# Graph layers over a 4096 by 4096 matrix: spills moved from SyncE's queue to GpSimd's, late loads placed between them, quadrants loaded in the order 0, 2, 1, 3

## The reference, cut to what matters

```python
def reference(x, adj, L0_gnn_W, L0_gnn_B, L1_gnn_W):      # x 4096x128, adj 4096x4096, W 128x128, float32
    h = max(layernorm(x), 0)
    msg = h @ L0_gnn_W + L0_gnn_B
    sens = exp(-(1/adj - 1)**2 / 0.5)                     # mu = 1, sigma = 0.5
    x = x + where(adj < 1, sens, 0) @ msg                 # first layer: every block of adj, weighted
    h = max(layernorm(x), 0)
    A = adj + I
    d = sum(A, axis=1) ** -0.5                            # row sums of adj
    x = x + relu((d[:, None] * A * d[None, :]) @ (h @ L1_gnn_W.T))   # second layer: every block again
    return x
```

## Time and profile before

| | us |
|---|---|
| median of 3 runs | 627.53 (626.89 to 627.85) |
| the profiled execution's own time | 632.89 |
| its span in the trace | 631.1 |

### The profile page before, as it was taken

One profiled execution on the slowest core, in us unless ns is written; L12 is line 12 of the kernel. 1 busy time (PEld: TensorE's weight loads), 2 busy tenths in 40 slices (PEclk: granted clock), 3 DMA queues, 4 the chain that ended last, 5 costly groups with the idle time before them and its releaser, 6 DMA issues.

```text
span 631.1 us, 4420 instructions
## 1 busy us (share of the span) xinstructions
PE 537.5 (85%) x1509; PEld 243.6 (39%) x1509; DVE 485.1 (77%) x555; ACT 466.0 (74%) x306; POOL 39.6 (6%) x68
## 2 busy tenths in 40 slices
PE   2446896969877998779769999979999999999995
PEld 2133432323322443334324444434444444444442
DVE  2799977789759899989989979986799849202056
ACT  2286878789967969999999969992999777920010
POOL 0241500000000000000000000000000000101100
PEclk9997998879888999989979999979999999999998
DMA  7999999999999959999999999999699951295623
GB/s 151 197 277 272 277 335 278 277 265 245 313 300 265 202 102 303 307 233 188 306 304 201 203 212 282 270 266 197 236 224 219 233 126 67 93 376 226 236 60 75
DMA packets 87193, 145.14 MB, mean 230 GB/s; under 512 B 4225, under 2 KB 78210, under 8 KB 78210
## 3 DMA queue, kind: packets, MB, share of 16 engines
q1 hardware_dynamic: 82130, 108.15, 75.2%
q0 software_dynamic: 5040, 36.70, 16.2%
HBM read 106.04 MB, written 38.80 MB: 230 GB/s over the span
## 4 chain that ended last, share of the span: by engine, by line
PE 42%; DVE 21%; ACT 14%; DMA 12%; issue 7%; SPq 4%; DVEq 0%
PE acc L377 13%; DMA raw<-in_adj_dram 12%; PE mix L399 11%; PE mix L390 11%; DVE kept L648 9%; DVE wt L663 4%; ACT wt L528 3%; ACT wt L533 3%; ACT wt L538 3%; SPq L281 3%; ACT wt L547 3%; DVE wt L669 2%; DVE rowpart L656 2%; PE acc L399 2%; PE side L399 1%
## 5 line engine op out<-in xcount | busy, mean ns | idle before, releaser
L377 PE MATMUL acc<-wt,msg 128*128 128x512 f32 x512 | 242.0, 617 | 4.7 <-ACT wt L547 4.7
L648 DVE STREAM_TRANSPOSE kept<-raw 128x2048 f32<-128x2048 f32 x64 | 147.6, 2306 | 42.9 <-DMA raw<-in_adj_dram 31.4
L377 PEld LDWEIGHTS acc<-wt,msg 128*128 128x128 f32 x512 | 98.6, 199 | 134.1 <-issue 124.3
L528 ACT ACTIVATE wt<-wt 128x2048 f32<-128x2048 f32 x64 | 121.9, 1905 | 38.1 <-DVE wt L663 38.1
L663 DVE SCALAR_TENSOR_TENSOR wt<-kept 128x2048 f32<-128x2048 f32 x64 | 146.5, 2288 | 1.5
L533 ACT ACTIVATE wt<-wt 128x2048 f32<-128x2048 f32 x64 | 121.6, 1900 | 0.4
L390 PE MATMUL mix<-kept,support 128*128 128x512 f32 x224 | 106.2, 620 | 13.0 <-DVE kept L648 6.5
L547 ACT ACTIVATE wt<-wt 128x2048 f32<-128x2048 f32 x52 | 98.8, 1899 | 0.0
L538 ACT ACTIVATE wt<-wt 128x2048 f32<-128x2048 f32 x52 | 98.7, 1898 | 0.0
L399 PE MATMUL mix<-late,support 128*128 128x512 f32 x200 | 89.7, 592 | 0.0
L656 DVE TENSOR_REDUCE rowpart<-raw 128x16 f32<-128x4096 f32 x20 | 87.6, 4379 | 0.0
(11 more groups left out here) (87 smaller groups left out, 260.8 us busy)
## 6 DMA issues: line engine op xcount, KB each, us to landing
raw<-in_adj_dram SPq DMA_DIRECT2D x128, 512.0 KB, 12.5
adj_t_spill<-kept SPq DMA_DIRECT2D x35, 1024.0 KB, 13.4
late<-adj_t_spill POOLq DMA_DIRECT2D x27, 1024.0 KB, 10.9
raw<-adj_t_spill POOLq DMA_DIRECT2D x8, 1024.0 KB, 6.2
x<-in_x_dram SPq DMA_DIRECT2D x32, 64.0 KB, 7.5
out_dram<-kept SPq DMA_DIRECT2D x32, 64.0 KB, 1.8
w_sb<-in_L_gnn_W_dram SPq DMA_DIRECT2D x1, 64.0 KB
late<-in_L_gnn_W_dram SPq DMA_DIRECT2D x1, 64.0 KB
```

The source lines that it names most:

```text
L377: mm = nc.tensor.matmul(acc0[:], msg[:, col(u) * T + k, :], wt[:, u % WTS, k, :], start=(first and k == 0), stop=(last and k == T - 1))
L528: nc.scalar.activation(v, v, ACT.Ln, bias=LN_GUARD).then_inc(ln_done, 1)
L648: nc.vector.transpose(dst, src).then_inc(turned, 1)
```

## The change

Three things. The spills leave SyncE's queue: GpSimd issues them, in the order of the units. SyncE's program keeps the loads of x, the adj loads and the stores of the result, and the loop over units becomes a plain loop over pairs; what an adj load waits for stays the same. GpSimd's program becomes a loop over the units: the spill of unit u, then (at units 0, 2 and 4) a portion of `support`, then those late loads whose `load_unit` is u. `load_unit(j)` is two units behind the unit at which PE takes the job that had the buffer before, and 16, 17 and 18 for the first three late loads, which have no job before them. The four quadrants of a pair are issued in the order 0, 2, 1, 3 in place of 0, 1, 2, 3. No arithmetic changes and no bytes are added.

```diff
@@ new helpers
+def load_unit(j):
+    before = slot_before(j)
+    if before is None:
+        return 2 * G + j
+    return first_unit(before) + 2
+
+def first_unit(j):
+    return [u for u in sorted(JOBS) for _ in JOBS[u]][j]
@@ SyncE
-                for q in range(Q):
+                for q in (0, 2, 1, 3):
                     sp.dma_start(raw[q * B:(q + 1) * B, n % RAW], ...
-            for u in range(UNITS):
-                if spills(u):
-                    sp.wait_ge(turned, u + 1)
-                    store(u)
-                if u % 2 == 1 and u // 2 + RAW < PAIRS:
-                    load(u // 2 + RAW)
+            for n in range(RAW, PAIRS):
+                load(n)
@@ GpSimd
+            def store(u):
+                pool.wait_ge(turned, u + 1)
+                pool.dma_start(spill[u // G, col(u)], ...).then_inc(spilled[u % KEPT], 16)
-            for j, (r, c) in enumerate(LOADED):
+            for u in range(UNITS):
+                if spills(u):
+                    store(u)
+                if u in (0, 2, 4):
+                    make_h0(u // 2 + 1)
+                for j in range(len(IN_TURN)):
+                    if load_unit(j) == u:
+                        load_late(j)
+            for j in range(len(LOADED)):
+                if j >= len(IN_TURN) or load_unit(j) >= UNITS:
+                    load_late(j)
```

## The result

| | us |
|---|---|
| before, median of 4 runs | 627.61 (626.89 to 627.85) |
| after, median of 4 runs | 639.88 (636.11 to 641.68) |
| ratio, 95% interval | 1.0179 (1.0136 to 1.0222) |
| profiled execution, before and after | 632.89 and 641.68 |

What follows compares the result with a forecast made beforehand. DMA was taken to bound the kernel up to unit 38, then PE and ACT. Terms -4.7 and +1.6 gave -3.1 us, so the median 627.53 becomes 624.4; forecast's range 620.5 to 626.2, 8 in 10 612 to 637.

Steps and rivals of the forecast that it cites:

- What bounds the kernel: Whole kernel: DMA sets the pace through transposes and adj loads up to unit 38 (323 us), then PE and ACT.
- a us is a us: Up to unit 38: a us saved or lost at a transpose moves the end by a us.
- Part 1: First two late loads, moved behind units 16 and 17: load for unit 8 freed of 4.9 us, returning about 70 us later.
- Part 2: Quadrant order of adj loads: four rate rises per pair in place of two, 0.6 us less, 9.9 in place of 10.5.
- Part 3: Spills on their own queue: one more spill in front of each load, +2.5 us once; mixing price taken as 0.
- the term for groups 3 and 4: Loads for units 28, 32 and 38, where spills stop and begin again: +1.6 us, bounds 0 and +5.
- -4.7 was forecast for unit 24: Up to unit 22, kept by unit 24: 12 pairs at -0.6 us make -7.2, plus 2.5 for the extra spill.
- Crowding wins: Rival at adj loads beside spills up to unit 38: slower, 641 or 635 us; chance of slower in all 0.29.
- Of its two ways the second: The rival's case where the new order saves nothing and groups 3 and 4 cost 5 us: +7.5, so 635.

Runs made afterwards that it cites:

- experiment 1: The kernel before with only the quadrants in the order 0, 2, 1, 3, spills still on SyncE's queue: 622.57 us, ratio 0.9898.
- experiment 4: The kernel before with only the late loads' times changed to those of the changed kernel, spills still on SyncE's queue: 628.73 us, ratio 1.0003.
- experiment 6: The changed kernel with the 14 spills of groups 3 to 7 back on SyncE's queue in their old places: 627.87 us, ratio 0.9982.
- experiment 9: The kernel before with quadrant order 0, 2, 1, 3 and the 14 spills of groups 3 to 7 on GpSimd's queue: 632.86 us, ratio 1.0063.
- experiment 10: The changed kernel with spills issued by ScalarE on its own queue, late loads staying with GpSimd: 636.5 us, ratio 1.0123.
- experiment 11: The kernel before with quadrant order 0, 2, 1, 3 and the first four late loads held until units 12, 22, 23, 24 are transposed: 619.24 us, ratio 0.9822.
- experiment 7: The changed kernel with the spill area laid out so that spills and late loads move in pieces of 2 KB, not 8: 639.76 us, ratio 1.0166.

## Why the prediction was wrong, step by step

**What bounds the kernel: right up to unit 38.** Between before and after a us lost at a transpose up to there is one at the end: unit 40 is 8.8 us late and so is the last one, and the spans differ by 8.8. The exchange is not always one for one, though. The order alone gained 8.0 us at unit 38 and 10.3 at the end. PE at unit 38, before and then in experiment 1:

```profile
325.62 6.15 PE L390 MATMUL mix<-kept,support 128*128 128x512 f32 x8 [6.06 <-DVE kept L648]
317.63 3.70 PE L390 MATMUL mix<-kept,support 128*128 128x512 f32 x8 [1.46 <-DVE kept L648]
```

Before, PE had stood 6.06 us, its granted clock from 324 to 328 us was 0.50 (1.2 GHz), and eight matmuls took 6.15 us. In experiment 1 it had stood 1.46 us, the clock was 1.00 (2.4 GHz), and the same eight took 3.70. So some 2.4 us more hang on the wait before unit 38 than the wait itself, and "a us is a us" left this out. After pays it too (5.93 us), so it drops out of the 8.8. Experiment 4, whose profiled execution is near its median, doesn't pay it (3.70 us): its unit 38 is 0.7 us earlier than before and its end 4.0. The profiled execution of before, 5.4 us above its median, is thus partly slow for this, which is one reason why the profiled executions differ by 8.8 us and the medians by 12.3. Whether the other executions of before pay it is not known.

**Part 1: its own sum right, its setting wrong.** The wait of unit 8 went (-4.4 us in place of 4.9), and placing alone moves the time by nothing (experiment 4). But "over the whole DMA-bound stretch" assumed that the stretch stays bound by DMA. It did not: with the lead won, DVE set the pace and DMA time at 124 to 130 us went unused. And "come back about 70 us later" named the four late loads and not what they would meet: four spills in the same 20 us on the same queue, with the load for unit 20 in flight beside it. That was the wait of 16.25 us.

**Part 2: right in mechanism, too large per pair.** Predicted -7.2 us by unit 22; alone it measured -5.2 there, -6.1 at unit 24 and -8.0 at unit 38, and 6.3 us on the median (experiment 1: ratio 0.9898). The rise at every boundary is there; the mean rate alone is 206 GB/s, where 9.9 us a pair needs 212.

**Part 3: the step that failed.** "One more spill in front of each load than before: +2.5 us, once, not per pair, since every earlier load is moved by the same." The exchange rate behind it was right: packets go one for one (729 to 709 from 160 to 175 us), which leaves a load 49 GB/s, a quarter of its 200 where a fifth was said; turns of several pieces at a time, which would have halved the price, are not seen. The price of mixing was near the zero that was taken (29.0 us of work in 28). The count was wrong. "Once" holds where each load is issued early and only queues. It fails where a load is issued late, because it waits for its buffer or for row sums, and has a fixed hour to land. Before unit 30 the single queue let two spills run first in the gap (418 GB/s) and kept the next two behind the load; the second queue let those two cross it, 5.1 us by the rate and 5.5 by the trace. Unit 38 repeats it. The prediction priced the loads for units 28, 32 and 38 and never asked about that for unit 30; for unit 38 it counted one spill fewer in front, where two now cross. So the term for groups 3 and 4, +1.6 in the sum with bounds 0 and +5, measured +9; and it wasn't before unit 28, as said, but before units 30 and 38. The rest of the miss lies earlier: -4.7 was forecast for unit 24 and -0.2 came, which is the first loss and the smaller gain per pair. With both, -4.7 + 1.6 = -3.1 became -0.2 + 9.0 = +8.8.

**The sum by measured terms**, by ratios times 628: the order -6.4 (experiment 1); spills of groups 0 to 2 on a second queue with the late loads among them +5.3 (experiment 6 less experiment 1); spills of groups 3 to 7 on it +10.4 (experiment 9 less experiment 1). In all +9.3, where the ratio 1.0179 makes +11.2. With the other half of groups 3 to 7, after less experiment 6 (+12.4), the sum closes by itself and proves nothing, so the 2 us between are the error of adding parts, and lie within the intervals. The rival "Crowding wins" gave the right side and nearly the time (635 and 641), by luck, with a mechanism that is hardly there: at 150 to 178 us the mixing had no price, and from 160 to 175 rather a gain (5.17 / 0.414 + 0.73 / 0.200 = 16.1 us of work in 15). Only from 248 to 256 us, where the load for unit 30 begins, do the rows leave room for one (0.76 / 0.414 + 1.10 / 0.200 = 7.3 us of work in 8). Of its two ways the second, the upper bound in groups 3 and 4, was the nearer. What the rows of before could have told: SyncE's order shows spills behind every load in flight, so the question at each late-issued load was "which transfers that stood behind it will now cross it?", and not how many spills there are in front on average.

**Open.** Why the order gives 3.3 us in the changed kernel and 6.3 in the old (the two runs of the changed kernel can't tell 3.3 from a gain near 6 or near none; the clock at unit 38 may be a part, since experiment 1 escapes its price and after doesn't); and how the 3.4 us between experiment 10 and after divide.

## What to carry to other kernels

The order of transfers in one first-in-first-out queue is a priority: a transfer behind a load can use the gap after it but doesn't slow it down (before, with two spills queued behind it, the load for unit 30 moved some 1.55 MB in 8 us; beside them, 1.10). Before moving transfers to a second queue, list for each load with a deadline which of them stood behind it and will now cross it, and charge their whole time to it. Deferred transfers go where the trace shows the DMA engines at rest or the next deadline far off, and not in a row with others (experiment 11). And read shares of two queues only in a window in which both have work: over a longer one the mean mixes sharing with running alone.

## What the runs showed of the hardware

Alternating the halves of the 128 partitions between transfers of one queue raised the mean rate of adj loads in flight alone from 200 to 206 GB/s, some 3% (by slices of 2 us; at best from 200 to 230, experiment 1, 200 to 214.5 us), and is worth 1% of the kernel's time. The Trainium skill, "SBUF — State Buffer", section "Can I just issue two DMAs to hit both halves?", has two such transfers at once 6% faster than one; the mean here is less, the best stretch more.

Queues that all have work take equal turns, packet by packet, with packets of 1, 4 and 8 KB alike: 729 packets of 1 KB to 709 of up to 8 KB (after, 160 to 175 us), 1136 to 1136 of about 4 KB (experiment 7, same window), and 140 to 136 to 133 among three queues (experiment 10, 160 to 165 us). So a load of 1 KB pieces keeps 49 GB/s beside one queue of 8 KB pieces, 75 beside one of 4 KB packets and 28 beside two of 8 KB.

PE that had stood 6.06 us for unit 38 ran the next eight matmuls in 6.15 us at a granted clock of 0.50, and after 1.46 us of standing in 3.70 at 1.00 (before and experiment 1).
